# A recommender's interaction tower: eight of batch 0's nine one-hot fields by products, one by gathers, and other work between the second and the third Gram chunk

## The reference

```python
e = stack([tbl_f[ids[:, f]] for f in range(26)], axis=1)          # 2048 x 26 x 128
combined = concatenate([e, dense_x[:, None, :]], axis=1)           # 27 rows a sample
interact = einsum('bfd,bgd->bfg', combined, combined)              # 27 x 27 Gram matrix
z = interact[:, triu_i, triu_j]                                    # 351 pairs above the diagonal
h = concatenate([z, dense_x], axis=1)                              # 479
h = maximum(h @ W_top1 + b_top1, 0)                                # 512
h = maximum(h @ W_top2 + b_top2, 0)                                # 256
y = h @ W_top3                                                     # 1
```

## Time and profile before

| | us |
|---|---|
| median of 3 runs | 385.13 |
| lowest, highest | 384.95, 386.6 |
| the profiled execution | 386.03 |
| its span, first to last instruction | 384.2 |

### The profile page before, as it was taken

How to read it: one execution, slowest core, us unless ns; L and a number is a source line. 1 busy time by engine, 2 the same in 40 slices (tenths; PEclk the granted TensorE clock), 3 DMA queues, 4 the chain that set the end, 5 groups by cost and what they waited for, 6 DMA issues and landing times.

```text
span 384.2 us, 12018 instructions
## 1 busy us (share of the span) xinstructions
PE 334.0 (87%) x5327; PEld 242.1 (63%) x5327; DVE 233.0 (61%) x389; ACT 186.9 (49%) x281; POOL 270.8 (70%) x288
## 2 busy tenths in 40 slices
PE   4999599778688989888998999988997899899776
PEld 3677477566576656557676666557676454578665
DVE  6889799687885829276896929467793011303030
ACT  6587634544515345345444434356444454655323
POOL 7777777777777777777777777777777777777100
PEclk9999989989989999989999999999999999989699
DMA  7998233433332423413343332423212221222000
GB/s 188 255 256 232 77 89 90 99 77 86 82 89 76 86 74 82 111 51 90 77 106 86 85 80 62 119 66 85 78 54 52 56 57 50 57 57 53 19 4 2
DMA packets 24195, 33.61 MB, mean 87 GB/s; under 512 B 6527, under 2 KB 17538, under 8 KB 24144
## 3 DMA queue, kind: packets, MB, share of 16 engines
q0 software_dynamic: 8960, 18.37, 18.2%
q1 hardware_dynamic: 15184, 14.48, 16.1%
HBM read 32.82 MB, written 0.01 MB: 85 GB/s over the span
## 4 chain that ended last, share of the span: by engine, by line
PE 54%; POOL 19%; issue 11%; DVE 7%; ACT 4%; DMA 3%; POOLq 0%; SPq 0%; DVEq 0%; ACTq 0%
POOL gat L372 19%; PE prod L431 12%; PE prod L433 11%; PE gram L460 8%; PE back L502 6%; PE front L405 5%; PE back L506 4%; DVE ring L708 4%; PE back L492 2%; ACT ct L600 1%; DVE ring L702 1%; DMA oh_last<-in_tbl,idx 1%; DMA gat<-in_tbl 1%; PE prod L417 1%; PE back L487 1%
## 5 line engine op out<-in xcount | busy, mean ns | idle before, releaser
L372 POOL DMA_INDIRECT gat<-in_tbl,idx x272 | 260.8, 959 | 83.0 <-issue 81.8
L708 DVE TENSOR_SCALAR ring<-idb,rowid 125x516 fp32r<-125x516 int32 x216 | 145.9, 741 | 16.9 <-PE prod L433 16.6
L431 PE MATMUL prod<-ring,tab_hi 125*128 125x512 f32 x264 | 110.0, 417 | 6.9 <-DVE ring L708 3.8
L433 PE MATMUL prod<-ring,tab_lo 125*128 125x512 f32 x264 | 106.1, 402 | 0.0
L600 ACT COPY ct<-front 128x512 f32<-128x512 f32 (+2 forms) x80 | 72.7, 964 | 25.0 <-PE front L405 22.6
L715 DVE COPY z<-gram 128x216 f32<-128x216 f32 x32 | 12.2, 382 | 111.1 <-PE gram L460 111.1
L460 PE MATMUL gram<-ct 128*32 128x27 f32 x4096 | 56.1, 196 | 17.1 <-issue 9.9
L460 PEld LDWEIGHTS gram<-ct 128*32 128x32 f32 x4096 | 46.7, 109 | 34.1 <-issue 24.8
L431 PEld LDWEIGHTS prod<-ring,tab_hi 125*128 125x128 f32 x264 | 51.4, 195 | 22.8 <-issue 8.4
L433 PEld LDWEIGHTS prod<-ring,tab_lo 125*128 125x128 f32 x264 | 51.2, 194 | 10.2
L405 PE MATMUL front<-ident,gat 128*128 128x128 f32 x272 | 42.7, 283 | 9.7 <-ACT ct L600 3.8
(11 more groups left out here) (73 smaller groups left out, 226.8 us busy)
## 6 DMA issues: line engine op xcount, KB each, us to landing
idb<-in_ids_t SPq DMA_DIRECT2D x27, 258.0 KB, 4.1
gat<-in_tbl,idx POOLq DMA_INDIRECT x272
oh<-in_tbl SPq DMA_DIRECT2D x3, 448.0 KB
oh<-in_dense_t SPq DMA_DIRECT2D x4, 256.0 KB, 3.1
gat<-in_tbl SPq DMA_DIRECT2D x2, 448.0 KB
h<-in_tbl SPq DMA_DIRECT2D x2, 448.0 KB
w1z<-in_w SPq DMA_DIRECT2D x1, 702.0 KB
w2s<-in_w SPq DMA_DIRECT2D x1, 512.0 KB
```

The costliest lines, as they stand in the source:

```text
L372: nc.gpsimd.indirect_dma_start(out=gat[:, t % GS, i, :], out_offset=None, in_=tables[GATHERED[i]][:, :], in_offset=bass.IndirectOffsetOnAx ...
L431: nc.tensor.matmul(prod[:, :], tab_hi[0:OH_P, m, k, :], ring[0:OH_P, k, 0:SB], start=(k == 0), stop=False)
L433: nc.tensor.matmul(prod[:, :], tab_lo[0:OH_P, m, k, :], ring[0:OH_P, k, 0:SB], start=False, stop=(k == OH_K - 1)).then_inc(used, 1)
L708: nc.vector.tensor_scalar(ring[0:OH_P, k, :], idb[0:OH_P, n % IDB, :, 0:IW], rowid[0:OH_P, k:k + 1], None, ALU.is_equal).then_inc(built, 1)
```

## The change

`NX` becomes 1: of the nine one-hot fields of batch 0, eight are products now, and one is gathered in each of tiles 0 to 3. POOL has 276 gathers and not 280. In batch 0 the fills of a tile also come in another order: the first fill has the 17th field and the extra one, and POOL gathers these two first. A new step H does half a product (four chunks of the ring). In tiles 1 to 3 one field is cut in such halves, one before and one after the first two Gram chunks. In tiles 4, 5, 7, 8, 9 and 11 a field or a layer block is moved between the second and the third Gram chunk. In tiles 3, 7 and 11 ACT places the next tile's columns after the third chunk. DVE's chunks ahead come two, one, two, one in tile 0 and six after the second Gram chunk in all others that have any.

At the end, the fifth fill of tile 15 goes before the fourth block of job E; E's second block of the second layer goes behind the transposes of tile 15, and its third layer behind the tail's first layer. The tail's second and third layers run over the input blocks outside and the output blocks inside, each waiting only for the input block it takes. E's and the tail's results are stored together.

```diff
-NX = 2
+NX = 1
...
+    def halves(m, h):
+        return [("H", b + 1, m, h)]
...
-        return (S[0:4] + A[0:1] + S[4:5] + A[1:2] + S[5:6] + T[0:1] + A[2:3] + S[6:7] + T[1:2] + A[3:4] + T[2:3]
-                + A[4:5] + T[3:4] + A[5:6] + T[4:5] + A[6:7] + [("P", 0)] + O[0:1] + G[0:1] + PL + G[1:2] + O[1:2] + G[2:4])
+        return (S[0:4] + A[0:1] + S[4:5] + A[1:2] + S[5:6] + T[0:1] + A[2:3] + S[6:7] + T[1:2] + A[3:4] + S[7:8]
+                + T[2:3] + A[4:5] + T[3:4] + A[5:6] + T[4:5] + A[6:8] + [("P", 0)] + O[0:1] + G[0:1] + PL + G[1:2] + O[1:2] + G[2:4])
...
     if t == TILES - 1:
-        return T[0:1] + N[4:5] + T[1:2] + N[5:6] + T[2:3] + Z + T[3:4] + N[6:7] + E[0:4] + T[4:5] + G + E[4:7]
+        return T[0:1] + N[4:5] + T[1:2] + N[5:6] + T[2:3] + Z + T[3:4] + N[6:7] + E[0:3] + T[4:5] + E[3:4] + G + E[4:5]
...
     if u == 1 and b == 0:
-        return T[0:2] + O[2:3] + T[2:3] + Z + T[3:4] + O[3:4] + T[4:5] + G[0:1] + PL + G[1:4]
+        return T[0:2] + O[2:3] + T[2:3] + Z + T[3:5] + halves(3, 0) + G[0:1] + PL + G[1:2] + halves(3, 1) + G[2:4]
...
+        return T[0:2] + J[4:5] + T[2:4] + Z + T[4:5] + O[4:5] + G[0:1] + PL + G[1:2] + O[5:6] + G[2:4]
+    if b == 0:
+        return T[0:3] + O[6:7] + T[3:4] + Z + O[7:8] + T[4:5] + halves(8, 0) + G[0:2] + halves(8, 1) + G[2:3] + PL + G[3:4]
+    return T[0:2] + J[5:6] + T[2:3] + O[6:7] + T[3:4] + Z + T[4:5] + O[7:8] + J[6:7] + G[0:2] + O[8:9] + G[2:3] + PL + G[3:4]
...
-END = [("Z", TILES - 1)]
+END = [("Z", TILES - 1), ("L", NB, 2, 1), ("L", NB, 3, 0)]
...
-    if t + 1 == TILES or not onehots_of(t + 1):
-        return 0, 0, 0, 0
-    steps = [s for s in tile_steps(t) if s[0] in "GO"]
-    return (0, 6, 0, 0) if steps[-3][0] == "O" else (2, 1, 2, 1)
+    return (2, 1, 2, 1) if t == 0 else (0, 6, 0, 0) if t + 1 < TILES and onehots_of(t + 1) else (0, 0, 0, 0)
...
-        def fill_columns(c):
-            return range(c * TCH, min((c + 1) * TCH, NG))
+        def fill_columns(t, c):
+            part = (c + TF - 1) % TF if t < BT else c
+            return range(part * TCH, min((part + 1) * TCH, NG))
         def extra(t, c):
-            return NX if t < BT and c == TF - 1 else 0
+            return NX if t < BT and c == 0 else 0
...
+            for job in range(NB - 1, len(JOBS) - 1):
                 store(job, JOBS[job])
-            store(len(JOBS), TAIL_JOB)
-            sp.wait_ge(y_out, 16 * (len(JOBS) + 1))
+            store(len(JOBS), (NB - 1, SB - 2 * P, SB))
+            sp.wait_ge(y_out, 16 * len(JOBS))
...
-            def onehot_products(b, m):
+            def onehot_products(b, m, chunks=range(OH_K)):
...
+                    elif kind == "H":
+                        b, m, h = q
+                        onehot_products(b, m, range(h * OH_K // 2, (h + 1) * OH_K // 2))
...
             turn_pairs(TILES - 1)
+            layer_step(*END[1][1:])
             pe.wait_ge(back_free, BACK_INDEX[("Z", TILES - 1)] + 1)
-            for i, (_, n, m) in enumerate(TAIL):
-                if n > 1:
-                    pe.wait_ge(tail_free, M1 if n == 2 else M1 + M2)
-                layer_block(tail_banks[i], TAIL_JOB, n, m).then_inc(tail_done, 1)
+            for m in range(M1):
+                layer_block(tail_banks[m], TAIL_JOB, 1, m).then_inc(tail_done, 1)
+            layer_step(*END[2][1:])
+            _, lo, hi = TAIL_JOB
+            for k in range(M1):
+                pe.wait_ge(tail_free, k + 1)
+                for m in range(M2):
+                    ins = nc.tensor.matmul(tail_banks[M1 + m][:, 0:P], w2s[:, k, m * P:(m + 1) * P], h1[:, k, lo:hi],
+                                           start=(k == 0), stop=(k == M1 - 1))
+                    if k == M1 - 1:
+                        ins.then_inc(tail_done, 1)
+            for k in range(M2):
+                pe.wait_ge(tail_free, M1 + k + 1)
+                ins = nc.tensor.matmul(tail_banks[M1 + M2][0:1, 0:P], w3s[:, k:k + 1], h2[:, k, lo:hi],
+                                       start=(k == 0), stop=(k == M2 - 1))
+            ins.then_inc(tail_done, 1)
```

More of the change, by code:

```diff
@@ L426, in onehot_products @@
                     pe.wait_ge(lo_ready, m + 1)
-                if n > 0:
+                if n > 0 and chunks[0] == 0:
                     pe.wait_ge(prod_free, n)
-                for k in range(OH_K):
+                for k in chunks:
                     pe.wait_ge(built, OH_K * n + k + 1)
```

31 lines of the change are left out of this document (17 added, 14 removed).

## The result

| | us | runs |
|---|---|---|
| before | 386.74 (384.56 to 391.62) | 17 |
| changed | 382.29 (380.4 to 384.77) | 17 |
| ratio | 0.9899, 95% interval 0.9877 to 0.9921 | |

The changed kernel is faster by 1.0%; 1.8% was forecast. 382.29 us lies above the range of 375.8 to 380.9. The profiled execution took 383.58 us with a span of 381.8, where the prediction had 379.0 for the execution. The 4.6 us between them are found with two marks. The last gather was forecast for 351.9 us and started at 353.17, and the fourth fill of tile 15 came at 354.44 and not at 353.2: **1.2 us too late**. From there to the end it took 27.4 us, not 23.9: **3.5 us too long**, and longer than the 26.6 us of before.

A forecast was written before the change was run, and what follows sets the result against it. The prediction took POOL's gather chain of 357.54 us plus a 26.6 us tail as the bound. Gains of 4.3 (gathers), 0 (PE) and 2.7 (tail) sum to 7.0 us, giving a median of 378.1 us, range 375.8 to 380.9.

The forecast's parts named there:

- Gathers as the bound: POOL's gather chain sets the time; four fewer at 1.249 us, less 0.7 for the eighth ring, bring the last 4.3 earlier.
- after 353 us, the ring: Sign of the rival that DVE's ring set blocks POOL throughout: first term 1.7 instead of 4.3, time 380.7; chance 0.06.
- Eighth product on PE: End of batch 0: the added product, net 3.5 us, hides where PE waited for DVE's ring; 0 us, bounds 0 and 3.5.
- Moved pieces: Reordered PE work: PE reaches the last meeting with at least 5.6 us less, but gathers stay the bound; 0 us.
- Fewer than four pauses before tile 15: Sign that the new order removes pauses called issue in Gram runs; the whole trace had nine before, 9.9 us.
- The tail: From tile 15's fourth fill to the end: reordered steps save 2.7 us, bounds 1.4 and 4.0, leaving 23.9 us.
- so PE still sets it: Tail, transposes of tile 15: PE arrives at 372.1, after DVE's pairs end at 371.6, so PE sets their start.
- I leave it so: Tail: TensorE's 6.8 us at 1.2 GHz stay as before; at full clock they would be some 2.5 us shorter.
- the pause is gone: Upper bound of the tail's gain, 4.0 us, if the 1.35 us pause behind tile 15's Gram run vanishes.
- PE as the bound: Rival: pauses stay and the eighth product costs 3.5 us, so the sum is 5.5 and the time 379.6; chance 0.12.
- The seams: Rival, slower than before: added Gram chunk boundaries in tiles 1 to 11 each cost a 1.2 us pause; 392.5 us; chance 0.02.
- The clock rival: Tail: one more slow stretch after a longer wait gives 379.8 us, none gives 375.6; chance 0.12 together.

The follow-up runs named there:

- e8: Kernel before with the eighth field of batch 0 done by a product and nothing else; 384.73 us, ratio 0.9944 to before.
- e12: Changed kernel with six extra product-like matmuls on PE just ahead of the wait for tile 15's fourth fill; 380.16 us, ratio 0.9864.
- e6: Kernel before with the change's new tail alone; 384.14 us, ratio 0.994 to before.
- e7: Changed kernel with the old tail, so all of the change but the tail; 383.96 us, ratio 0.994 to before.
- e5: Changed kernel, meant to have 128 empty instructions that its trace does not show, so taken as one more execution; 383.37 us beside 387.17.
- e10: Changed kernel once more, unaltered; 382.29 us, ratio 0.9892.
- e11: Changed kernel with 64 small unused matmuls ahead of everything on PE; median 382.67 us, ratio 0.9844 from the shortest three of its six executions.
- e1: Kernel before with the change's new tail alone, run where every kernel took 660 to 695 us; ratio 0.995.
- e9: Changed kernel with 32 small unused matmuls ahead of everything on PE; 380.11 us, ratio 0.9837.
- e4: Changed kernel's new order with NX = 2 (280 gathers) and the old tail, measured at about 680 us; ratio 1.0087.
- e18: Kernel before with seven small unused matmuls ahead of everything, the same kernel as e14 once more; 674.16 us against 672.83.
- e14: Kernel before with seven small unused matmuls ahead of everything on PE; 680.59 us, ratio 0.9994.
- e13: Changed kernel with tile 15's Gram run split around the fourth block of the last job; 379.58 us, ratio 0.983.

## Why the prediction was right or wrong

- *Gathers as the bound, 1.249 us each*: right. Every fourth fill of tile 15 waited for a gather in the executions at 385 us, 0.65 us at least with the change. Over nine profiled executions with 276 gathers the last one started at 352.7 us in the mean (351.5 to 354.4), over the two with 280 at 356.9. That is 4.2 us, forecast 4.3. The single execution came 1.3 us late by its long gathers. The mark "after 353 us, the ring" was met, and half rightly: it is not the eighth ring, which costs no more than the 0.7 worked out (e8 and e12, without long gathers, start their last one 4.5 and 4.7 us before that of the kernel before), but single gathers in any of the ring sets. It was so with 280 gathers too (e6: 1.68 us at 6.57, 2.47 at 37.62). In the eleven traces at 385 us there are 13 long gathers, none to three in each, and all ended 0.1 us after DVE's set. Such a gather behaves as if DVE took the exclusive lock that the Trainium skill describes (SBUF — State Buffer, Who interferes with whom) again and again to the end of its set. Read as a block for the whole set, the rule agrees with these 13 alone: the other gathers that began in a set, eleven or more in each trace, took 1.28 us or less. That is up to 0.34 more than usual, less than one of the set's eight instructions of 0.41 us, and so no contradiction to a lock held for one instruction.
- *Eighth product on PE, 0 us*: right (Gram chunk at 51.78 us, forecast 52).
- *Moved pieces, 0 us on the path*: right in its result (e7 against e8). The reserve can't be read from PE's coming to the last meeting, at 352.98 instead of 355.56, since it had waited for gathers ahead of it. Without all waits for gathers PE would have been there at 352.9 before, at 348.9 in the changed kernel and at 343.7 in e7: 4.0 and 9.2 us earlier, where 5.6 were forecast. "Fewer than four pauses before tile 15" held by count: there were three, of 1.07, 1.04 and 4.09 us. But the one of 4.09, in tile 5, is longer than any of before (1.5 at most) and takes back much of what the seams gained.
- *The tail, 2.7 us*: here the prediction failed. The tail was to take 23.9 us and took 27.4, 27.2, 26.9 and 26.7 in the four traces of the changed kernel's order with pauses at its places (the profiled one, e5, e10, e11). **The step that failed is the sum of the tail, with its pause of 1.35 us taken as standing behind the Gram run, its "so PE still sets it" of the transposes of tile 15, and its "I leave it so" of the clock.** Of the 3.1 us too many in the mean of the four, 1.2 are length of the pauses (2.1 to 3.3 us, typical with either count, where the one trace of before had 1.35). Another 1.2 are the order: the 13 more matmuls put the pause ahead of the run's last nine matmuls, DVE's pairs come after it, and DVE sets the transposes and not PE, so that the order gives 1.5 and not 2.7. The last 0.6 are the clock, 0.3 to 1.0 more than before. The prediction's own rows had DVE at 371.6 and PE at 372.1 with the pause of 1.35 between them; they left 0.5 us of room, and its upper bound of 4.0, "the pause is gone", overlooked the same. With the pause behind the run, as in e1 and e6, the order gives 3.0, so the moves themselves were priced well.
- *The base*: the median of before was 385.13 in three runs and is 386.74 in 17. Of the 4.2 us by which the median was missed, 1.6 are this, 2.6 the size of the change (4.4 us measured, 7.0 forecast). A range that took the base as known was too narrow by that alone.
- *Rivals*: PE as the bound is refuted. The seams cost nothing that shows. The clock rival (one more slow stretch, 379.8) happened in part: there is one more, at 366.6 us, but behind the pauses and not behind a longer wait, and the clock cost 0.3 to 1.0 us more where 1.7 were priced.
- *Open*: e8 has the 4.5 us in its gathers, and its median shows 1.9. Its ten runs fall into two groups (381.1 twice, 384.5 to 385.4 seven times, and one at 383.1); three of the seven have the clock of the two, 0.973, so there the difference is not the mean clock. Only one of the first was traced, and it had no long gather; that the others had some is possible (three cost e11 4.5 us) and not shown. Open too is why half clock follows the pauses in the changed kernel, e9, e12, e4 and e18, and not in e6, e7, e8 and e14, whose pauses are as long.

## What to carry to other kernels

When a pause or a wait in the middle of a chain is taken as standing, ask what other engine works during it: here DVE's 3.0 us for the pairs were hidden behind a pause, and 13 matmuls added 300 us earlier moved the pause so that they no longer were. Adding instructions anywhere moves the places at which a run of short ones pauses; in e13 a Gram run cut by a block of larger matmuls had one pause of 1.26 us in place of 2.1 to 3.3. Behind a wait, price both clocks: waits of 1.5 us or more ahead of the tail were followed each time by half clock, and with six matmuls of no use ahead of the wait that stretch ran at full clock. A term read from one execution needs its spread, and a base of three runs needs a term of its own in the range.

## What was not expected of the hardware

**The same program at 1.8 times the time.** In e1 to e4 and e14 to e18 PE pauses by the hundred; the waits list of e1 has, for Gram matmuls,

```profile
PE gram L461 <- issue: 223.9, 230, 2.6
```

against 9.9 us in nine pauses. The timeline of e14 shows what a Gram run looks like there:

```profile
569.80 0.18 PE L460 MATMUL gram<-ct 128*32 128x27 f32 x1 [0.50 <-issue]
570.51 0.20 PE L460 MATMUL gram<-ct 128*32 128x27 f32 x1 [0.52 <-issue]
571.23 0.20 PE L460 MATMUL gram<-ct 128*32 128x27 f32 x1 [0.52 <-issue]
572.66 0.26 PE L460 MATMUL gram<-ct 128*32 128x27 f32 x2 [1.22 <-issue]
```

One or two matmuls, then 0.5 or 1.2 us of nothing, for dozens of microseconds, but in tile 15 whole runs of 120 and 128 at full speed. POOL's gathers took their usual 0.94 us. Which shared part is slow no run tells. It need not belong to the chip: the record gives the number 9 for the chip of e5, at 383 us, and for that of e18, at 674.

**Single gathers of 1.67 to 3.21 us** during DVE's writing of a ring, in some executions and not in others (before, e8 and e12 had none, e7 one), between 6 and 47 us and each to the end of the set. What decides which gather it meets no run tells.
